# A delta-rule attention kernel: eviction of the refined inverse by an addition, half copies moved between engines, new instruction orders

## The reference, cut to what matters

```python
A = -jnp.where(strict_tril, jnp.einsum('bhnce,bhnde->bhncd', k_beta, kc) * decay, 0.0)
T = jax.scipy.linalg.solve_triangular(eye - A, jnp.broadcast_to(eye, A.shape), lower=True)
value_ = T @ v_beta
k_cumdecay = T @ (k_beta * jnp.exp(g)[..., None])
```

## Time and profile before

| | |
|---|---|
| median of 3 runs | 4884.31 us (4884.26 to 4885.98) |
| profiled execution | 4879.86 us |
| its span | 4878.1 us |
| mean granted TensorE clock | 0.986 |
| instructions | 131563 |
| DMA, mean over the span | 77 GB/s |

### The profile page before, as it was taken

One profiled execution on the slowest core, in us unless ns is written; L12 is line 12 of the kernel. 1 busy time (PEld: TensorE's weight loads), 2 busy tenths in 40 slices (PEclk: granted clock), 3 DMA queues, 4 the chain that ended last, 5 costly groups with the idle time before them and its releaser, 6 DMA issues. The chain is left out here.

```text
span 4878.1 us, 131563 instructions
## 1 busy us (share of the span) xinstructions
PE 4636.4 (95%) x38533; PEld 3256.8 (67%) x38788; DVE 4411.3 (90%) x9152; ACT 3901.1 (80%) x8976; POOL 2338.0 (48%) x1689
## 2 busy tenths in 40 slices
PE   5799999999999999999999999999999999999978
PEld 3566666676666666676666666676766666676653
DVE  4899999999999999999999999999999999999953
ACT  3788888888888888888888888888888888888842
POOL 2355554545455454545455454545455454545420
PEclk7899999999999999999999999999999999999988
DMA  4122222212222222222222221222222222222122
GB/s 154 64 73 80 66 87 70 87 65 77 76 75 81 65 87 70 86 66 76 76 75 82 65 87 65 89 68 75 77 73 84 65 87 65 86 71 73 64 78 82
DMA packets 185165, 377.26 MB, mean 77 GB/s; under 512 B 86400, under 2 KB 95744, under 8 KB 184960
## 3 DMA queue, kind: packets, MB, share of 16 engines
q1 hardware_dynamic: 185088, 376.46, 23.8%
HBM read 360.13 MB, written 16.25 MB: 77 GB/s over the span
## 5 line engine op out<-in xcount | busy, mean ns | idle before, releaser
L658 PE MATMUL p_proj<-hid,w_in 128*128 128x512 f32 x3072 | 1599.1, 609 | 28.8 <-POOL ident_h L1184 28.4
L1019 DVE SCALAR_TENSOR_TENSOR conv<-p_proj,taps,conv 128x509 f32<-128x509 f32 (+2 forms) x1536 | 1130.6, 736 | 42.2 <-ACT conv L885 33.4
L936 ACT ACTIVATE x_bd<-x_t 64x512 bf16<-64x512 bf16 x1280 | 801.3, 626 | 113.4 <-DVE x_t L1101 105.9
L1198 POOL TENSOR_TENSOR root<-sums,half_pow 128x8 f32<-128x8 f32 x128 | 210.8, 1647 | 1290.5 <-DVE sums L1029 1249.0
L658 PEld LDWEIGHTS p_proj<-hid,w_in 128*128 128x128 f32 x3072 | 526.8, 192 | 128.5 <-issue 65.8
L1094 DVE TENSOR_TENSOR y_h<-p_lev,y_h 128x512 bf16<-128x512 f32 x640 | 440.9, 689 | 151.8 <-PE p_lev L724 143.8
L971 ACT ACTIVATE g_t<-p_out 128x512 bf16<-128x512 f32 x256 | 152.8, 597 | 488.7 <-PE p_out L779 488.7
L867 PE MATMUL p_out<-h_t,w_out 128*128 128x512 f32 x1024 | 475.0, 607 | 44.5 <-DVE ga L1073 43.4
L1101 DVE STREAM_TRANSPOSE x_t<-y_h 128x512 bf16<-128x512 bf16 x640 | 449.9, 703 | 4.5
L1073 DVE SCALAR_TENSOR_TENSOR ga<-p_out,neg_c,dec 128x256 f32<-128x256 f32 x1024 | 422.4, 476 | 26.1 <-ACT dec L923 21.8
L1086 DVE TENSOR_TENSOR q_h<-p_lev,consts 128x512 bf16<-128x512 f32 x640 | 430.9, 673 | 1.8 <-PE p_lev L718 1.8
(11 more groups left out here) (212 smaller groups left out, 12101.6 us busy)
## 6 DMA issues: line engine op xcount, KB each, us to landing
w_in<-in_w_in SPq DMA_DIRECT2D x128, 768.0 KB, 4.8
g_row<-rows_scratch SPq DMA_DIRECT2D x128, 512.0 KB, 3.2
hid<-h_scratch SPq DMA_DIRECT2D x128, 512.0 KB, 5.8
e_row<-exp_rows_scratch SPq DMA_DIRECT2D x128, 512.0 KB, 3.7
w_out<-in_w_out SPq DMA_DIRECT2D x128, 256.5 KB, 2.7
x<-in_x SPq DMA_DIRECT2D x8, 512.0 KB, 10.2
h_scratch<-x SPq DMA_DIRECT2D x8, 512.0 KB, 2.6
y_scratch<-y_acc SPq DMA_DIRECT2D x8, 512.0 KB, 5.0
```

What stands on the lines that cost most here:

```text
L658: last = pe.matmul(p_proj[tile % 2][:], w_in[p][:, kt, tile * P:(tile + 1) * P], hid[p][:, kt, :], start=(kt == 0), stop=(kt == KT - 1))
L936: last = act.activation(x_bd[block, :, block], x_t[block], ACT.Copy)
L1019: dve.scalar_tensor_tensor(conv[:, tile, late:], p_proj[tile % 2][:, 0:S - late], taps[p][:, tile, j:j + 1], conv[:, tile, late:], ALU.mul ...
```

## The change

W loses its identity product, and IV, now on VectorE, adds `x_dn` to the bank. XB's first half stays on ScalarE, its second half is an `affine_select` on GpSimd that keeps partitions 64 to 127 and writes zero in the others. AB, s (now YB) and p go from VectorE to ScalarE. XD waits for IV in place of W. All four orders are new.

```diff
-PE_ORDER = ("ON1@1 Y1@3 U0@2 P10@3 M2@3 KS1@2 P11@3 O0@2 Y2@3 VT0@3 TR1@2 M3@3 P0@4 P1@4 Y3@3 U1@2 O1@2 M4@3 W1@2 "
-            "KS2@2 P2@4 Y4@3 P3@4 TR2@2 M5@3 VT1@3 P4@4 U2@2 P5@4 KS3@2 Y5@3 O2@2 KT@4 QT@4 XD@3 Q6@3 TR3@2 P6@4 "
-            "Z6@3 P7@4 D0@3 XC@3 D1@3 O3@2 KK0@4 KK1@4 P8@4 OY0@1 OY1@1 G0@3 L@4 G1@3 W0@3 M1@4 P9@4 TR0@3 ON0@2")
-ACT_ORDER = ("XB1@1 SV0@1 SV1@1 VX0@0 XB2@1 OT0@0 Z0@1 Z1@1 XB3@1 VX1@0 C0@2 VK0@1 XB4@1 OT1@0 OQ0@0 IV1@0 AO@1 "
-             "OQ1@0 C1@2 XB5@1 VX2@0 VK1@1 C2@2 SK@2 SQ@2 OT2@0 KN@2 QN@2 XD@1 VX3@0 KT@2 YC@1 GE@2 XC@1 OQ2@0 OT3@0 "
-             "OQ3@0 C3@2 v0@1 v1@1 IV0@1")
-DVE_ORDER = ("T7@3 SN2@2 F0@2 SM0@3 SM1@3 SM2@3 F1@2 SM3@3 T8@3 GA0@3 GA1@3 GA2@3 OS0@1 GA3@3 OS1@1 T9@3 YA0@0 AB0@3 "
-             "AB1@3 YA1@0 y0@3 T10@3 X1@3 q1@3 T11@3 VW0@2 HT0@1 y1@3 ST0@2 X2@3 q2@3 RR1@2 HT1@1 y2@3 X3@3 VW1@2 "
-             "q3@3 SN0@3 y3@3 ST1@2 X4@3 T0@4 q4@3 T1@4 RR2@2 y4@3 T2@4 X5@3 VW2@2 q5@3 T3@4 ST2@2 T4@4 SN1@3 T5@4 "
-             "y5@3 s10@3 s11@3 RR3@2 KN@4 p6@3 QN@4 T6@4")
-POOL_ORDER = ("OP@1 ON@1 QD@2 SD1@2 GL@4 AR@3 SD2@2 AL@3 PW@4 RL@3 SL@4")
+PE_ORDER = ("ON1@1 Y1@3 U0@2 O0@2 M2@3 VT0@3 P11@3 Y2@3 KS1@2 W1@2 M3@3 TR1@2 P0@4 Y3@3 U1@2 P1@4 M4@3 O1@2 KS2@2 "
+            "Y4@3 VT1@3 P2@4 M5@3 TR2@2 P3@4 Y5@3 U2@2 O2@2 Q6@3 KS3@2 XD@3 P4@4 KT@4 P5@4 QT@4 Z6@3 TR3@2 P6@4 P7@4 "
+            "D0@3 O3@2 D1@3 KK0@4 XC@3 KK1@4 P8@4 OY0@1 OY1@1 G0@3 P9@4 L@4 W0@3 P10@4 M1@4 G1@3 TR0@3 ON0@2")
+ACT_ORDER = ("VX2@0 C1@2 YB@1 p6@1 SK@2 XD@1 OT2@0 SQ@2 KN@2 C2@2 YC@1 QN@2 KT@2 VX3@0 GE@2 OQ2@0 OT3@0 OQ3@0 C3@2 "
+             "XC@1 AB@2 v0@1 SV0@2 v1@1 XB1@2 VX0@1 SV1@2 XB2@2 OT0@1 AO@2 Z0@2 XB3@2 VK0@2 OQ0@1 VX1@1 Z1@2 C0@3 "
+             "XB4@2 OT1@1 OQ1@1 VK1@2 XB5@2")
+DVE_ORDER = ("GA0@3 GA1@3 GA2@3 OS0@1 GA3@3 OS1@1 T9@3 YA0@0 SN0@3 T10@3 T11@3 YA1@0 SN1@3 y0@3 IV0@2 X1@3 q1@3 "
+             "VW0@2 HT0@1 y1@3 ST0@2 X2@3 q2@3 HT1@1 y2@3 RR1@2 X3@3 q3@3 VW1@2 IV1@2 y3@3 ST1@2 X4@3 q4@3 T0@4 "
+             "RR2@2 y4@3 X5@3 q5@3 VW2@2 T1@4 y5@3 T3@4 ST2@2 T2@4 T4@4 T5@4 RR3@2 KN@4 T6@4 QN@4 T7@4 T8@4 SN2@3 "
+             "F0@3 SM0@4 SM1@4 SM2@4 SM3@4 F1@3")
+POOL_ORDER = ("RL@2 SL@3 OP@1 ON@1 XB1@3 XB2@3 XB3@3 SD1@2 AR@3 XB4@3 SD2@2 XB5@3 QD@3 GL@4 AL@3 PW@4")
...
@@ PE, Y: waits for the second half too; W: no identity product @@
                     t.wait(pe, "xbd", n)
+                    t.wait(pe, "xbd_low", n)
...
-                    pe.matmul(p_out[n][:], ident_h[:], quarter(x_dn, n).rearrange("p a i -> p (a i)"),
-                              start=True, stop=False)
                     for u in range(n * 4, n * 4 + 4):
-                        pe.matmul(bank(n)[:, u - n * 4, :], r_lo[:, u, :], x_dn[:, u, :], start=False, stop=False)
+                        pe.matmul(bank(n)[:, u - n * 4, :], r_lo[:, u, :], x_dn[:, u, :], start=True, stop=False)
...
@@ ScalarE @@
-                    for block in (slice(0, HB), slice(HB, P)):
-                        last = act.activation(x_bd[block, :, block], x_t[block], ACT.Copy)
-                    last.then_inc(s["xbd"], 1)
+                    act.activation(x_bd[0:HB, :, 0:HB], x_t[0:HB], ACT.Copy).then_inc(s["xbd"], 1)
                 elif name == "XD":
                     t.wait(act, "xt6")
-                    t.wait(act, "w_mm", back=1)
+                    t.wait(act, "inv_done", back=1)
...
+                elif name == "AB":
+                    t.wait(act, "strict")
+                    t.wait(act, "q_mm", back=1)
+                    for block in (slice(0, HB), slice(HB, P)):
+                        last = act.activation(a_bd[block, :, block], ga[p][block, :, 0, block], ACT.Copy)
+                    last.then_inc(s["abd"], 1)
+                elif name == "YB":
+                    t.wait(act, "y_done")
+                    t.wait(act, "xt6", back=1)
+                    t.wait(act, "xt7", back=1)
+                    t.wait(act, "d_mm", back=1)
+                    for block in (slice(0, HB), slice(HB, P)):
+                        last = act.activation(y_dn[block, :, block], y_h[block], ACT.Copy)
+                    last.then_inc(s["ydn"], 1)
+                elif name == "p":
+                    t.wait(act, "q6_mm")
+                    t.wait(act, "z6_mm", back=1)
+                    act.activation(p_h[HB:P], p_lev[HB:P, :].rearrange("p (u f) -> p u f", f=HB), ACT.Copy)\
+                       .then_inc(s["p6_done"], 1)
...
-                elif name == "IV":
-                    t.wait(act, "w_mm", n + 1)
-                    t.wait(act, "tr_mm", back=2)
-                    act.activation(quarter(inv_t[p], n), bank(n), ACT.Copy).then_inc(s["inv_done"], 1)
...
@@ VectorE: AB, s and p go; y0 waits for YB of the step before, X for the second half; IV comes @@
+                elif name == "IV":
+                    t.wait(dve, "w_mm", n + 1)
+                    t.wait(dve, "tr_mm", back=2)
+                    dve.tensor_tensor(quarter(inv_t[p], n), bank(n), quarter(x_dn, n), ALU.add).then_inc(s["inv_done"], 1)
...
@@ GpSimd @@
+                elif name == "XB":
+                    t.wait(pool, "xt_done", n)
+                    if n == 1:
+                        t.wait(pool, "y_mm", back=1)
+                    else:
+                        t.wait(pool, "y_mm", n - 1)
+                    pool.sem_inc(passed, 1)
+                    pool.affine_select(x_bd[:, :, HB:P], x_t[:], [[0, U], [0, HB]], ALU.is_ge, zero,
+                                       base=-HB, channel_multiplier=1).then_inc(s["xbd_low"], 1)
```

More of the change, by code:

```diff
@@ L451, in attention @@
                       k_sum=1, q_sum=1, rooted=1, scaled=4, w_scaled=1, q_scaled=2, g_low=1, decay=1, kk_mm=2, ga_done=4,
-                      strict=1, aoff=1, abd=2, rest=1, alo=1, q_mm=6, q_done=5, y_mm=5, y_done=6, xt_done=5, xbd=5,
-                      ydn=2, xt6=1, xdn=1, q6_mm=1, p6_done=1, z6_mm=1, y21=1, xt7=1, x12=1,
+                      strict=1, aoff=1, abd=1, rest=1, alo=1, q_mm=6, q_done=5, y_mm=5, y_done=6, xt_done=5, xbd=5, xbd_low=5,
+                      ydn=1, xt6=1, xdn=1, q6_mm=1, p6_done=1, z6_mm=1, y21=1, xt7=1, x12=1,
                       d_mm=2, r_done=2, rlo=1, g_mm=2, g_done=2, w_mm=2, inv_done=2,
@@ L791, in emit @@
                                           (0, ("v_tok_done", None)), (1, ("inv_done", None)))
-                    pe.matmul(p_out[n][:], ident_h[:], quarter(x_dn, n).rearrange("p a i -> p (a i)"),
-                              start=True, stop=False)
                     for u in range(n * 4, n * 4 + 4):
-                        pe.matmul(bank(n)[:, u - n * 4, :], r_lo[:, u, :], x_dn[:, u, :], start=False, stop=False)
+                        pe.matmul(bank(n)[:, u - n * 4, :], r_lo[:, u, :], x_dn[:, u, :], start=True, stop=False)
                         pe.matmul(bank(n)[:, u - n * 4, :], top(resid[:, u, :]), x_dn[:, u, :], start=False, stop=False)
-                        last = pe.matmul(bank(n)[:, u - n * 4, :], top(resid[:, u, :]), g_t[:, u, :], start=False,
-                                         stop=(u == n * 4 + 3))
+                        last = pe.matmul(bank(n)[:, u - n * 4, :], top(resid[:, u, :]), g_t[:, u, :], start=False, stop=True)
                     last.then_inc(s["w_mm"], 1)
@@ L1075, in emit @@
                     last.then_inc(s["ga_done"], 1)
[L1076 to L1079, removed]
                 elif name == "q":
@@ L1090, in emit @@
                     t.wait(dve, "q6_mm", back=1)
+                    t.wait(dve, "ydn", back=1)
                     dve.tensor_tensor(y_h[:], levels(), each(const["mask"][:, 0:HB], U), ALU.mult).then_inc(s["y_done"], 1)
@@ L1098, in emit @@
                         t.wait(dve, "xbd", back=1)
+                        t.wait(dve, "xbd_low", back=1)
                     else:
                         t.wait(dve, "xbd", n - 1)
+                        t.wait(dve, "xbd_low", n - 1)
                     dve.transpose(x_t[:].rearrange("p u f -> p (u f)"), y_h[:].rearrange("p u f -> p (u f)"))\
                        .then_inc(s["xt_done"], 1)
[L1103 to L1112, removed]
+                elif name == "IV":
+                    t.wait(dve, "w_mm", n + 1)
+                    t.wait(dve, "tr_mm", back=2)
+                    dve.tensor_tensor(quarter(inv_t[p], n), bank(n), quarter(x_dn, n), ALU.add).then_inc(s["inv_done"], 1)
                 elif name == "F":
@@ L1185, in _ @@
             pool.wait_ge(init, 1)
-            minus_one = pool.to_reg(-1.0)
+            minus_one, zero = pool.to_reg(-1.0), pool.to_reg(0.0)
             def emit(name, t, n):
```

## The result

The changed kernel takes 5043.61 us (median of 4 runs, 5042.29 to 5046.57) against 4884.28 in the same session: ratio 1.0326 [1.0308, 1.0344], slower by 159 us. The profiled execution has a span of 5042.8 us. The forecast was 5026, slower.

What follows compares the result with a forecast made beforehand. In-order queues form one cycle of 35.43 us a step, VectorE nearly full. Queues alone give 34.85, plus 1.7 for the held SN1: 36.55, 1.12 more, x 127 = +142 us, so 5026 us; range 4800 to 5065.

Steps and rivals of the forecast that it cites:

- The hold: VectorE's small SN1, before y0, is held to the end of GpSimd's ON: 1.7 us a step; chance 0.58.
- Nothing takes this back: After SN1, y0's road to y1 and y5's road to `ga` are dependencies, so the whole 1.7 us stays.
- The road over `g_t` and XB1: From y0 to y1 by M1, G1, `g_t`, XB1, Y1: claimed as long as VectorE's own 3.44 us.
- The queues: In-order engine queues alone, without the hold, give a step of 34.85 us, 0.58 less than now.
- the three cuts: The step's cycle split at `ga`, y1 and y5's end, each stretch summed separately.
- `ga` to y1: First stretch of the step, in VectorE's new order: y1 at 10.39 us against 10.54 now.
- y1 to y5's end: The solve: 16.93 us falls by 3.56 to 13.4, with 1.0 from shorter level-product waits.
- y5's end to `ga`: Last stretch, set by ScalarE: 0.05 plus 11.0 us, where it was 7.96.
- Not held: Rival: SN1's form escapes or it gets in before ON; 34.85 us a step, -74 us, 4810; chance 0.32.
- The select: GpSimd's lower half of x_bd takes 0.6 us, each level 0.6 shorter; rival that it is the bound: 0.05.
- SN0: Small VectorE instruction in the first stretch, falling on the power's first reads on GpSimd: costs 0 to 0.1 us.
- ScalarE's chain: Behind y5, YB and p lengthen it from 8.56 to 11.0 us, gapless to `dec`; it becomes what is late.

Runs made afterwards that it cites:

- e1: Changed kernel with only SN1 (VectorE's product of inv with inv) moved from before y0 to behind HT0, out of GpSimd's ON: 4882.9 us, ratio 0.9996 to before.
- e4: Kernel before with SN1 moved from between T4 and T5 to between T10 and X1, where GpSimd's ON runs: 4969.1 us, ratio 1.0172.
- e2: Changed kernel with SN1 in its place and with its waits, but made a reciprocal of root, one SBUF input: 4875.6 us, ratio 0.9981 to before.
- e8: Kernel before with only the identity product removed and IV made an addition on VectorE: 4961.5 us, ratio 1.0162.
- e7: e1 with both halves of XB on ScalarE again, nothing of it on GpSimd: 5158.3 us, ratio 1.0559 to before.
- e9: Kernel before with only XB's lower half made a select on GpSimd, and SN0 moved next to SN1: 4863.3 us, ratio 0.9968.
- e6: e1 with YB's two y_dn copies back on VectorE, behind y5: 5578.5 us, ratio 1.1419 to before.

## Why the prediction was right, point by point

**The hold.** The mechanism was right, and so was the margin: SN1 at 6.78 us after the first `ga` against 6.83 forecast, y0 at 8.47 against 8.7. It missed ON's start by 0.14 us (0.2 forecast), and as SN1 also waits for OP's two instructions in front of ON (done at 2016.95 + 0.20 = 2017.15), it could only have slipped in between 2017.15 and 2017.33. That the row is held by ON is shown three ways: e1 takes it away, e4 puts it into the kernel before, e2 leaves place and waits as they are. Its price was mis-sized: 1.32 us a step (36.81 - 35.49), not 1.7. "Nothing takes this back" was wrong: y0 moves by 1.65, y1 by only 1.30. Without the hold VectorE's own queue from y0 to y1 has gaps and SN1 in it, 0.35 in all (under e1), and the hold covers these. The road over `g_t` and XB1 isn't the later one into y1 in e1, as y1 starts right behind SN1.

**The queues.** Without the hold I forecast 34.85; e1 has 35.49. By the three cuts:
- `ga` to y1: 10.39 forecast, 10.55. y0 came 0.13 earlier than summed (6.82 against 6.95, with SN1 no longer ahead of it), y0 to y1 took 3.73 against 3.44: IV0's wait for W0, 0.17 beyond its 0.61, and SN1's 0.07 are most of that.
- y1 to y5's end: 13.4 forecast, 35.49 - 11.48 - 10.55 = 13.46. The additions take 675 ns in the changed kernel (0.69 forecast), and the waits for level products are gone.
- y5's end to `ga`: 11.05 forecast, 2020.37 - 2008.89 = 11.48. Most of this is a slip that the earlier trace rows already showed: `dec` ends 0.29 before `ga`, and the sum ends at `dec`. In e1 it is 2020.37 - 2020.13 = 0.24. The other 0.2 is gaps: YB starts 0.03 after y5's end, and the chain from YB to `dec`'s end has 11.21, not 11.0.

So 0.64 too little and 0.38 too much: +0.26 a step, 33 us. The total is only 18 us off, since the first and last steps, what lies outside them and the scatter of the runs took 16 back. The closeness of 5026 to 5044 is in part luck: two of its terms were off with opposite signs, and so was what lies outside them.

**The gain without the hold.** "Not held" was priced at 4810; e1 and e2 show that it would have been 4883 or 4876: the change's queue side was to pay 74 us and pays nothing or hardly more. By the three cuts, e1 against before: `ga` to y1 10.55 and 10.54, y1 to y5's end 13.46 and 16.93, y5's end to `ga` 11.48 and 7.96. What the solve gains, 3.47 us, the stretch behind y5 with its longer ScalarE chain gives back, 3.52. Of the parts, e8 shows 0.64 us a step lost to the additions in the old order, and e7 2.15 gained by the halves in the new one.

**The select.** 0.66 us (0.6 forecast), and it hides: the `y_h` waits are gone, and e7 shows 2.15 us a step for it in this order. The prediction put those waits down to XB's length and gave PE's new order no term. e7 and e9 show that neither removes them alone: a wrong attribution inside a right sum.

**SN0.** At 2015.29, on the power over 8 elements (2015.22 to 2016.87), it took 0.16: not held, as forecast.

**ScalarE's chain.** It became the bound as forecast, gapless behind y5 but for hundredths, with `ga` waiting for `dec` and VectorE idle 1.4 + 0.5 us for squares.

## What to carry to other kernels

When an order is laid anew, look at every small SBUF-to-SBUF instruction of VectorE against GpSimd's long rows: for the forms that were held here its price is not its own duration but what is left of the GpSimd instruction, and it falls on whatever is queued behind it, on other engines too. In e6 this reached TensorE, whose clock then fell, so two held copies cost more than their own 3 us. A wait for a product names the engine that came last, not the reason; look at what that engine had queued ahead before pricing the operand's earlier arrival. Make the sum of a cycle close on the row that it began with, for a gap at a seam is a term too.

## What the hardware showed unexpectedly

- Behind a running GpSimd tensor_tensor that reads SBUF, a four-column VectorE instruction took 1773 ns (scalar_tensor_tensor, two SBUF inputs) and 1780 ns (tensor_scalar, one), but 171 ns as a reciprocal of another SBUF tile; a cast from PSUM kept its 0.69.
- GpSimd's power over 8 elements takes 1.65 us, more than its affine_select over 512 bf16 elements (0.66). The instructions of VectorE seen within it kept their durations: 0.88 for two casts, 0.16 for SN0, which has two SBUF inputs.
- 3.9 us without a TensorE instruction in each step (e6) came before a fall of the granted clock from 1.00 to 0.50. In the step shown it was still 0.50 up to 2015, with work since 2010.42, and the transposes took 1.06 us in place of 0.61.
